# Moving a stage's opening work into the stage before it, and reordering the opening of the next stage

## The reference

```
x = x + cross_attention(layernorm(x), ctx)     # 16 heads, 1024 context rows of width 128 per sequence
x = x + causal_self_attention(layernorm(x))    # 32 query heads, 4 key/value heads of width 64
x = x + mixture_of_experts(layernorm(x))       # 16 experts, 4 chosen per token, and a shared one
```

## Time and profile before

| | us |
|---|---|
| three runs of the kernel before | 1482.55, 1485.21, 1486.15 (median 1485.21) |
| the profiled execution, whole | 1482.78 |
| its span, first to last instruction | 1480.7 |
| PE busy over the span | 1349.8 (91%) |
| DVE, ACT, POOL busy | 800.2, 729.6, 577.0 |
| mean granted TensorE clock | 0.961 of 2.4 GHz |

### The profile page before, as it was taken

One profiled execution on the slowest core, in us unless ns is written; L12 is line 12 of the kernel. 1 busy time (PEld: TensorE's weight loads), 2 busy tenths in 40 slices (PEclk: granted clock), 3 DMA queues, 4 the chain that ended last, 5 costly groups with the idle time before them and its releaser, 6 DMA issues. The chain is left out here.

```text
span 1480.7 us, 22809 instructions
## 1 busy us (share of the span) xinstructions
PE 1349.8 (91%) x7136; PEld 1105.5 (75%) x7136; DVE 800.2 (54%) x1372; ACT 729.6 (49%) x1736; POOL 577.0 (39%) x350
## 2 busy tenths in 40 slices
PE   5998699999999999999985999998889989999991
PEld 4776477878787878787864888887678768787771
DVE  4434366666666666666654444445389843433245
ACT  2444366565656565656543677777321213343330
POOL 2430143323242414141103333334347396327975
PEclk9998799999999999999997999999799999999995
DMA  5785414141515141412041243442633156536767
GB/s 211 250 274 175 175 45 155 51 177 42 184 42 184 42 184 42 184 42 114 1 171 59 82 133 107 135 135 99 230 129 133 71 199 223 184 107 227 246 197 220
DMA packets 78984, 209.79 MB, mean 142 GB/s; under 512 B 5888, under 2 KB 39168, under 8 KB 72960
## 3 DMA queue, kind: packets, MB, share of 16 engines
q1 hardware_dynamic: 69472, 163.78, 32.0%
q0 software_dynamic: 7136, 38.80, 7.9%
q10 hardware_dynamic: 2304, 6.29, 1.1%
HBM read 154.59 MB, written 92.01 MB: 167 GB/s over the span
## 5 line engine op out<-in xcount | busy, mean ns | idle before, releaser
L745 DVE TENSOR_TENSOR probsT_lo<-psTr,probsT_hi 128x512 fp32r<-128x512 f32 x256 | 176.7, 690 | 166.2 <-ACT probsT_hi L698 165.9
L698 ACT CAST probsT_hi<-psTr 128x512 fp32r<-128x512 f32 x256 | 150.2, 587 | 197.0 <-PE psTr L835 193.3
L835 PE MATMUL psTr<-ident,probs 128*128 128x128 f32 x1024 | 153.6, 274 | 12.1 <-DVE probsT_lo L745 6.0
L835 PEld LDWEIGHTS psTr<-ident,probs 128*128 128x128 f32 x1024 | 124.1, 141 | 51.4 <-DVE probsT_lo L745 14.7
L740 DVE TENSOR_REDUCE nmax<-psS 128x1 f32<-128x1024 f32 x128 | 155.5, 1215 | 9.3 <-PE psS L81 8.2
L606 POOL TENSOR_TENSOR w_slots<-ctx_f,w_slots 128x512 fp32r<-128x512 f32 x32 | 41.4, 1294 | 279.4 <-ACT w_slots L657 279.4
L650 ACT ACTIVATE probs<-psS,nmax 128x1024 f32<-128x1024 f32 x128 | 143.7, 1123 | 12.1 <-DVE nmax L740 12.1
L79 PE MATMUL psS<-w_slots 128*128 128x512 f32 x256 | 113.0, 441 | 3.8 <-DMA w_slots<-qe 2.9
L79 PE MATMUL psV<-probsT_hi,w_slots 128*128 128x512 f32 x256 | 114.8, 449 | 0.7
L79 PE MATMUL bank<-w_slots,ao_first_hi 128*128 (+1 forms) x244 | 103.5, 424 | 6.1 <-POOL w_slots L1589 3.0
L1589 POOL TENSOR_TENSOR w_slots<-w_ahead,w_slots 128x3072 fp32r<-128x3072 f32 x15 | 102.2, 6812 | 1.2
(11 more groups left out here) (287 smaller groups left out, 3310.2 us busy)
## 6 DMA issues: line engine op xcount, KB each, us to landing
w_ahead<-w_exp POOLq DMA_DIRECT2D x14, 1536.0 KB, 7.4
qe<-stage SPq DMA_DIRECT2D x16, 1024.0 KB, 6.8
w_slots<-qe SPq DMA_DIRECT2D x16, 1024.0 KB, 5.0
wraw<-w_pairs SPq DMA_DIRECT2D x8, 1792.0 KB, 11.2
early<-xs SPq DMA_DIRECT2D x47, 256.0 KB, 2.7
xs<-h_rows SPq DMA_DIRECT2D x47, 256.0 KB, 2.0
early<-ctx SPq DMA_DIRECT2D x16, 512.0 KB, 11.1
ao<-attn_out SPq DMA_DIRECT2D x32, 256.0 KB, 2.9
```

The lines of the kernel that those rows point to most:

```text
L698: act.copy(PT[k % PTN].hi[:], psT[slot][:]).then_inc(turned_hi, 1)
L745: dve.tensor_tensor(out, psT[slot][:], f32(hi), ALU.subtract).then_inc(turned_free, 1)
L835: last = pe.transpose(psT[slot][:, q * P:(q + 1) * P], src(q), ident[:])
```

## The change

Stage 1 gets the opening work of stage 2. The four key turns of sequences 0 and 1 are done in the last pair's step, in psT and psC, which no fold needs any more: PE turns 0 and 1 behind the Q product, 2 and 3 behind the two E products, with their ACT and DVE parts between the parts of Q, E and F. SP loads the folded queries of sequence 0 for pairs 0 to 6 from `qe` when pair 6's stores have landed and the last Q product is done (h1T, which lies where QE and KT go, is then free). POOL copies the last pair's part for sequence 0 from `stage`. SP no longer waits for the last stores in stage 1; in stage 2, SP waits for them before it loads sequence 1, and DVE before its first row maximum (the probabilities and `stage` share SBUF).

Stage 3 opens with all three remaining splits of W_qkv and with the four products (keys and values, groups 0, 1, 2) in a row; the turns come behind them. On ACT, the values and the second query group are copied before the exponentials of group 0 instead of behind them. On DVE, the values' low part and the terms of group 2 come before the first maximum.

```diff
@@ stage 1, SP
-        for j in range(2):
-            step(NP - 2 + j, j, False)
-        sp.wait_ge(stage_out, 32 * (NP + 1))
+        step(NP - 2, 0, False)
+        sp.wait_ge(q_mm, 2 * NP)
+        sp.wait_ge(stage_out, 32 * NP)
+        sp.dma_start(f32(QE[:, :, 0:(NP - 1) * 2 * S]),
+                     qe_d[:, 0, :, 0:NP - 1, :].rearrange("a d p x -> d a (p x)")).then_inc(qe_in[0], 16)
+        step(NP - 1, 1, False)
@@ stage 1, POOL
+        pool.wait_ge(q_mm, 2 * NP)
+        pool.wait_ge(e_free, 4 * NP + 2)
+        pool.tensor_copy(QE[:, :, (NP - 1) * 2 * S:], stage_o[:, :, 0]).then_inc(qe_tail, 1)
@@ stage 1, ACT
+        def key_high(q):
+            act.wait_ge(turned, q + 1)
+            act.copy(KT[q // 2].hi[:, q % 2 * BANK:(q % 2 + 1) * BANK], psK[q % 2][:]).then_inc(turned_hi, 1)
...
             if ahead:
                 fold_t(p + 1)
+            else:
+                key_high(0)
+                key_high(1)
             act.wait_ge(stage_out, 32 * p + 32)
...
+                if not ahead:
+                    key_high(2 + jj)
@@ stage 1, DVE: key_low(0), key_low(1) behind Q's low parts, key_low(2 + jj) behind E's
@@ stage 1, PE
+        def key_turn(q):
+            if q >= 2:
+                pe.wait_ge(turned_free, q - 1)
+            for a in range(BANK // P):
+                at = (4 * (q % 2) + a) * P
+                last = pe.transpose(psK[q % 2][:, a * P:(a + 1) * P], kr[q // 2][:, at:at + P], ident[:])
+            last.then_inc(turned, 1)
...
+            else:
+                pe.wait_ge(keep["rope_done"], 3)
+                key_turn(0)
+                key_turn(1)
             pe.wait_ge(wB_ready, p + 1)
...
+                if not ahead:
+                    key_turn(2 + jj)
@@ stage 2
-        for j in range(2):
-            load_qe(j, j)
+        sp.wait_ge(stage_out, 32 * (NP + 1))
+        load_qe(1, 1)
...
+        dve.wait_ge(stage_out, 32 * (NP + 1))
         for rt in range(RT):
             maxes(0, 0, rt)
...
-        pe.wait_ge(rope_done, 3)
-        for q in range(2):
-            turn_k(q, 0, q)
-        for q in range(2):
-            pe.wait_ge(turned_free, 3 + q)
-            turn_k(q, 1, q)
+        pe.wait_ge(turned_free, 2 + FIRST)
         pe.wait_ge(qe_in[0], 16)
+        pe.wait_ge(keep["qe_tail"], 1)
@@ stage 3, ACT
         high(2)
+        high(3)
         act.wait_ge(tab_in, 32)
         act.copy(mask, mask_f[:]).then_inc(consts, 1)
         act.copy(ident_r, ident[:]).then_inc(consts, 1)
-        high(3)
+        high(4)
         act.wait_ge(zeroed, 6)
+        v_high(0, VB[0])
         turned(order_k(0), KB[0], HKV)
         turned(order_q(0, 0), QB[0], REP)
+        turned(order_q(0, 1), QB[1], REP)
         exps(0, 0)
-        turned(order_q(0, 1), QB[1], REP)
-        v_high(0, VB[0])
-        high(4)
@@ stage 3, DVE
         low(2)
+        low(3)
         dve.wait_ge(tab_in, 32)
         terms_k(0)
+        low(4)
         terms_q(0)
-        low(3)
         terms_q(1, psO[:])
+        v_low(0, VB[0])
+        terms_q(2, psP[:].rearrange("p h t -> p (h t)"))
         dve.wait_ge(keep["x1_out"], 16 * NT + 16)
         maxes(0, 0)
-        v_low(0, VB[0])
-        terms_q(2, psP[:].rearrange("p h t -> p (h t)"))
-        low(4)
         recips(0, 0)
@@ stage 3, PE
         product(0, 0, 1, 2, psO[:], q_mm)
+        product(0, 0, 1, 3, psP[:].rearrange("p h t -> p (h t)"), q_mm)
         turn_k(0)
         turn_q(0, 0, 0)
-        product(0, 0, 1, 3, psP[:].rearrange("p h t -> p (h t)"), q_mm)
```

More of the change, by code:

```diff
@@ L186, in build_queries @@
     f_mm, f_hi, f_free = sem("f_mm"), sem("f_hi"), sem("f_free")
-    stage_out = sem("stage_out")
+    stage_out, qe_in, qe_tail = keep["stage_out"], keep["qe_in"], keep["qe_tail"]
+    turned, turned_hi, turned_free = keep["turned"], keep["turned_hi"], keep["turned_free"]
+    kr = keep["kv_rope"]
+    KT = [Shared(keep["ws"], AT_KEYS + 2 * j * L, (L,)) for j in range(2)]
+    QE = shaped(keep["ws"][:, AT_QE:AT_QE + 2 * H * S], (2, H * S))
+    psK = [psT, psC]
     def kq(w, j, qt):
@@ L344, in _, with key_low @@
                 fold_c(0)
+        def key_low(q):
+            dst = KT[q // 2]
+            cols = slice(q % 2 * BANK, (q % 2 + 1) * BANK)
+            dve.wait_ge(turned_hi, q + 1)
+            dve.tensor_tensor(dst.lo[:, cols], psK[q % 2][:], f32(dst.hi[:, cols]),
+                              ALU.subtract).then_inc(turned_free, 1)
         def step(p, ahead):
@@ L351, in step @@
                                   ALU.subtract).then_inc(q_ready, 1)
+            if not ahead:
+                key_low(0)
+                key_low(1)
             for jj in range(2):
@@ L359, in step @@
                     fold_c(p + 1)
+                if not ahead:
+                    key_low(2 + jj)
             for jj in range(2):
@@ L509, in build_cross @@
     kv_in, xt_in, rope_done = keep["kv_in"], sem("xt_in"), keep["rope_done"]
-    qe_in = [sem(f"qe_in{j}") for j in range(2)]
+    qe_in, stage_out = keep["qe_in"], keep["stage_out"]
     kv_hi, kv_lo = sem("kv_hi"), sem("kv_lo")
-    turned, turned_hi, turned_free = sem("turned"), sem("turned_hi"), sem("turned_free")
+    turned, turned_hi, turned_free = keep["turned"], keep["turned_hi"], keep["turned_free"]
     recip_made, rows_made = sem("recip_made"), sem("rows_made")
@@ L680, in turned_k @@
             act.copy(KT[j].hi[:, q * BANK:(q + 1) * BANK], psT[slot][:]).then_inc(turned_hi, 1)
-        for q in range(2):
-            turned_k(q, 0, q, q + 1)
-        for q in range(2):
-            turned_k(q, 1, q, q + 3)
         kv_high(0, 0)
@@ L2135, in build @@
         keep["rope_tab"] = early[:, 1].rearrange("p (a x) -> p a x", a=2)
-        for name in ("tab_in", "kv_in", "rope_part", "rope_done", "fill_in", "x1_out", "h2_out", "wqkv_hi", "wqkv_ready"):
+        for name in ("tab_in", "kv_in", "rope_part", "rope_done", "fill_in", "stage_out", "qe_tail", "turned",
+                     "turned_hi", "turned_free", "x1_out", "h2_out", "wqkv_hi", "wqkv_ready"):
             keep[name] = sem(name)
-        for name, n in (("ht_in", 2), ("wqkv_in", HQ // REP + 1), ("wo_in", W_AHEAD + 1), ("a_in", 2),
+        for name, n in (("qe_in", 2), ("ht_in", 2), ("wqkv_in", HQ // REP + 1), ("wo_in", W_AHEAD + 1), ("a_in", 2),
                         ("ao_out", 2)):
```

## The result

The changed kernel is faster. Its four runs were 1462.52, 1467.53, 1468.76 and 1469.15 us (median 1468.14) against a median of 1483.88 of four runs of the kernel before: ratio 0.9884, 95% interval 0.9865 to 0.9904, that is 17.2 us (14.2 to 20.0). The ratio and its interval are estimated from the single runs; the quotient of the two medians is 0.9894, 15.7 us. The forecast was 20.3 us. Profiled a second time, beside other kernels on another occasion, the ratio was 0.9883 (0.9861 to 0.9906). The profiled execution took 1467.53 us, with a span of 1465.5.

What follows compares the result with a forecast made beforehand. The kernel was taken as bound by PE in the long loops, with the change touching only the seams: 10.3 us at the first plus 10.0 at the second, 20.3 off 1485.2, gave 1464.9 us, range 1460 to 1473.5.

Steps and rivals of the forecast that it cites:

- Work moved into the last pair: End of stage 1: the moved key turns cost PE at most 3.9 us; PE enters stage 2 at 149.2 instead of 154.2.
- First maximum at the landing of the stores: Opening of stage 2: DVE waits for stores landing at 153.8, first row maximum at 153.9 instead of 164.51, 10.6 us earlier.
- right at the landing of the last stores, near 154: Sign to look for at the opening of stage 2: when the first row maximum should come in the new trace.
- From there to the fourth exponential: Stage 2, after the first maximum: fourth exponential starts at 161.1 (fast PE) or 162.6 (slow), 11.1 or 9.6 us earlier; 10.3 taken.
- the slow case: Opening of stage 2: third and fourth score tiles at 1.2 GHz, fourth exponential at 162.6, 9.6 us earlier.
- Transport: Stage 2 behind its opening: waits are on other engines or loads following them, so the shift carries to the stage's end.
- Second seam: Opening of stage 3: turn closing the first loop step 11.6 us earlier with fast PE, 9.2 with slow; 10.0 taken.
- past 790: Sign against the seam's term, opening of stage 3: ACT standing beyond 790 us for chunk 4 of W_qkv.
- back in under 5 us each time: Claim in the slower-clock rival (chance 0.03): PE's clock falls to 1.2 GHz at such places but recovers that quickly.
- The port rule: Stage 3 opening: DVE's split locks out POOL's sum (3.24 us against 1.29); in the new order no split lies beside a sum.
- One seam gives only part: Rival: late stores or late chunk 4 load cut the gain to 16 or 10 us, 1469 to 1475; chance 0.20, late entry included.
- Stage 2 enters late: Rival: PE still enters at 154.2, first seam gives 7.3 us, time 1468; chance 0.20 shared with a partial seam gain.

## Why the prediction was right, and where its terms were off

*Total.* 20.3 us were forecast and 17.2 measured, 1468.1 against 1464.9. The mechanism was right at both seams and the sum was a sixth too large.

*Work moved into the last pair.* As counted. The turns cost PE 0.6 to 0.7 us each and the last one 1.1, F's last low part ended at 148.2 (147.8 before, with a start 0.5 us earlier), PE entered stage 2 at 148.8, forecast 149.2. The new load was there in 4.8 us and nobody waited for it.

*First maximum at the landing of the stores.* Right in kind: DVE stood 6.98 us for exactly these. The size was off: "it might push them by 0 to 1.5 us; I take 0" looked at the new load, which was through before they started. Nearly all of the 1.8 us came from an instruction page: the eight profiles with a 16 KB page inside the stores have 9.7 to 10.5 us, the six without have 8.8 to 9.2, and three of these six have the change in them (8.9, 8.9, 9.2). So the landing at 153.8 is the term that was mis-sized, and the sign "right at the landing of the last stores, near 154" came true in its first half only.

*From there to the fourth exponential.* Forecast 7.2 (fast) or 8.7 us (slow), taken in the middle; it was 8.8, slow, with a stop of 4.59 us ahead of it. The term was 10.3 and measured 7.8: of the 2.5 missing, 1.8 are the stores and about 0.7 that the slow case came and not the middle. The experiment with the moved wait shows that both hang on one wait.

*Transport.* Through stage 2's loop nothing was lost. At its end 0.5 us was: the last turn ran at half clock (1.12 against 0.66 us).

*Second seam.* Forecast 10.0, measured 10.0 in the first trace and 11.6 in the second, but two errors met. Chunk 4 was counted for 788 at the latest as before; it took 7.6 us and the first query turn came 1.1 late (forecast 14.1 us behind PE's first matmul, measured 15.2). Two of the prediction's own signs show it: ACT began chunk 4 at 782.5, which is 790.3 in the times of before ("past 790"), and the first maximum lay 20.3 us behind the opening in place of 18.5, more than the 1.5 us allowed. The clock was better than the half-slow one that I had taken (0.88 granted from 788 to 802 us), so that the 10.0 of the first trace is in part luck. Also, the clock did not come "back in under 5 us each time" in the kernel before: the granted clock rose from 0.50 to 1.00 at 166.15, 4.6 us behind the matmul at 161.55, and at 818.1, 6.0 us behind the one at 812.07. Why the load takes 5.3 us once and 8.3 another time stays open. In the changed kernel one packet stood 1.9 us, then a 16 KB page came 4.9 us behind the issue, and the last packets followed one after another until 782.2, as at the stores. But the kernel before also had a page at 4.7 and 4.9 us and its chunk landed in 5.3 and 5.5, and of the five profiles without a page here two took 6.6 and 7.2.

*The port rule.* POOL's sum took 1.26 us with no split beside it, so the 3.24 of the row before came from the split beside it. The Trainium skill's page "SBUF — State Buffer", section "Who interferes with whom", calls this an exclusive lock; by that rule, the trace agrees.

*Rivals.* "One seam gives only part" was the nearest: the stores did land late, by another cause, and so did chunk 4. "Stage 2 enters late" did not happen, and yet the fetch of code was the thing to look at: not as a stop of the engine that fetches, but as traffic that holds up a transfer. The Trainium skill's page "Runtime: NRT & Kernel Launch", section "Instruction fetch mechanics", tells of code in 16 KB blocks fetched through a DMA queue of the sequencer's own; the 16 KB packets of these traces, on a queue that carries nothing else, agree; the pages on a second such queue have 8 KB.

*Stage 4.* The prediction has no term for it, and 2.4 us went there in the first pair of traces. Over fourteen profiles it took 324.8 to 331.1 us. The two of the kernel before have 327.2 and 328.3, the two of the changed one 329.8 and 329.2; the three with small matmuls 324.8 to 326.3, and that with 95 idle turns 327.4. Whether the place of the pages does this, or chance, stays open.

## What to carry to other kernels

Where a stage ends on a store and the next begins on a load of the same data, start the load before the last part and copy that part on chip; then ask what else waits for the store, and put that wait at the first instruction that writes over the stored memory, on the engine that does. Here that one wait, a few instructions too early, cost 5.5 us, beside the 7.5 to 7.9 that the seam gave with it. Work that only a later step needs (here the splits of W_qkv) can fill the time in which an engine would wait. But while its own data is still on its way, it belongs behind everything that does not need that data.

## What the runs showed of the hardware

A 16 KB instruction page took 0.9 to 1.0 us at the first seam, and the 2 MB of stores landed later with it than without: 8.8 to 9.2 us without such a page, 9.7 to 10.5 with it, most where it came at the stores' very end. The delay can thus be longer than the page's own time (1.6 us in the changed kernel against the ones with 50 and 100 small matmuls); how the rest of it arises is not shown. Small work on PE is not priced by its columns: a 128x128 fp32 transpose took 0.115 us in a row of 28 and 0.139 in a row of 95, an fp32 matmul with 16 columns 0.43 us. The trace records that matmul as two of 0.21 us, each with a weight load, at a granted clock of 1.00, and the transpose as one.
